# Fused attention and feed-forward: q and k turned by VectorE, first-half row sums added by GpSimd, V's first store moved

## The chip, the cores and the metric

The kernel runs on one NeuronCore of one Trainium2 chip. The time is device microseconds (us) of one execution; the time before is 1375.58 us, the median of 3 runs (1372.02 to 1378.19).

Names used throughout: PE is TensorE, DVE is VectorE, ACT is ScalarE, POOL is GpSimd, SP is SyncE, which here only issues DMAs. PEld is TensorE's weight load.

## The reference

Two batches of 1024 tokens, 1024 channels, 32 heads of 32. The FFN branch is one product with the signs of a weight.

```
def _L0_attn_ref(hidden_states, Wqkv, q_ln_w, q_ln_b, k_ln_w, k_ln_b, Wout):
    qkv = jnp.einsum('bsd,ed->bse', hidden_states, Wqkv)
    qkv = jnp.clip(qkv, -CLIP_QKV, CLIP_QKV)
    q, k, v = jnp.split(qkv, [D_MODEL, 2 * D_MODEL], axis=-1)
    q = _layer_norm(q, q_ln_w, q_ln_b)
    k = _layer_norm(k, k_ln_w, k_ln_b)
    ...
    scores = jnp.einsum('bqhd,bkhd->bhqk', q, k) * scale
    scores = scores + slopes[None, :, None, None] * rel[None, None]
    scores = jnp.where(causal[None, None], scores, jnp.float32(-1e+30))
    probs = jax.nn.softmax(scores, axis=-1)
    out = jnp.einsum('bhqk,bkhd->bqhd', probs, v).reshape(B, S, D_MODEL)
    return jnp.einsum('bsd,ed->bse', out, Wout)
...
x = L0_attn_hidden_states
xn = _layernorm(x, axis=-1)
x = x + _L0_attn_ref(xn, ...) + _L0_ffn_ref(xn, ...)
```

## The kernel before

The engines run hand-written instruction lists, tied by semaphores; nothing reorders them. `ready(n)` is the count a semaphore has once item n is done, `slot_free(n)` the count at which item n may overwrite item n-2.

**Stages.** PE goes through five products of 16 token tiles each (128 tokens by 1024 outputs): F (the feed-forward), Q, K, V, and at the end the output product. Between V and the output product lies attention. A tile of Q, K or V is 48 matmuls of 512 columns (L1038) into two of four PSUM banks, so product t+2 can begin only once DVE has taken tile t out of its banks.

**The Q and K stages.** In step t, DVE clips product t out of PSUM (L899), computes its mean and variance (L830, L835), splits a piece of the next weight (`split_lo`, L823), and scales and shifts the tile to `u[p]` (L920, L923), for which it needs a factor from POOL (L588). PE then turns the tile, 8 transposes of 128x128 fp32 (`turn_qk`, L1085) that stand behind the next product in PE's list. ACT copies the turned tile to its high half `th` (L718) and stores it; DVE subtracts to get the low half `tl` (`turned_low`, L909), which SP stores (L420). Each store writes runs of 128 tokens, 256 bytes, into `q_scr` or `k_scr`, laid out [head, dim and half, token]. The first product of the next stage waits for the last `split_lo` (`w_lo`).

**The V stage.** DVE clips tile t into one of two buffers (`vst`), and SP stores it (`store_v`, L439); DVE's clip of tile t+2 waits for that store. In SP's list the first of these stores stands behind the loads of the first three stacks (L357). A stack holds what one group of 4 heads needs of q and k, 128 rows with halves, ALiBi terms and a row of maxima; it is loaded in 8 parts, in runs of 1 or 2 KB. The last four V products have the first group's maxima in between.

**Attention.** There are 16 groups (8 of 4 heads in each batch). A group has 12 chunks, c = 0 to 11: c = 0 to 3 are the keys t = 0 to 3 of the first half of the queries, with 512, 384, 256 and 128 columns; c = 4 to 11 are t = 0 to 7 of the second half. At each place (c, j), j a head, PE computes scores (L1169, with a mask product L1172 on the diagonal), then some items of the next group's maxima (L1108; DVE reduces them, L940 and L944; ring of 3 banks), and at places named by `PV_AFTER` the product of an earlier chunk with V (L1192, 4 heads side by side, fp32) and with a matrix of ones (L1197), which gives the softmax's row sums in PSUM. ACT takes the exponential (L760) into one of four slots `p32`, used in turn. In the second half four chunks (t = 1, 2, 3, 5) aren't multiplied with ones: POOL adds them up in `acc` (L619), and one product with ones (L1202) closes the sum. ACT copies the product and the sums out (`os_copy`, L768, L769), SP sends the sums through DRAM for DVE's reciprocal, POOL multiplies (`o_norm`, L598), ACT and POOL split into halves (`o_high` L778, `o_low` L608). Two rows of maxima per group are turned on PE, copied by DVE, and put into the stack by SP (L444, L448). ACT issues the loads of the stack of group n+2 and of V.

## Time and profile before

| | us |
|---|---|
| median of 3 runs (lowest, highest) | 1375.58 (1372.02, 1378.19) |
| the profiled execution | 1374.1 |
| its span in the trace | 1372.3 |
| PE busy in the span | 1330.4 (97%) |
| DVE, ACT, POOL busy | 772.8, 503.8, 481.3 |
| first transpose of a q tile starts at | 167.17 |
| first V product starts at | 510.20 |
| last product of V is clipped from | 705.79 |
| first output product starts at | 1199.66 |

A row of the timeline is start, length, engine, line, operation, output and input, and how many instructions it merges; in brackets is the engine's idle time ahead and what ended it. The chain of waits follows the work that ended last back from the end. A PE that is "busy" has a matmul in flight, so its share says little by itself: what counts is which wait ends last in a stage.

### The profile page before, as it was taken

What the parts mean: (1) busy time and instruction counts of PE and PEld (TensorE: products, weight loads), DVE (VectorE), ACT (ScalarE), POOL (GpSimd) and SP (SyncE); (2) the same over time, 40 slices, a digit from 0 to 9 for tenths busy, and PEclk for the clock granted to TensorE, in tenths of its full rate; (3) what the DMA queues carried; (4) which work ended last, traced back from release to release, by engine and by line L of the source; (5) the groups of instructions that cost most, each with busy time, mean ns of one, the idle gap of its engine ahead of it and who ended that gap; (6) DMA issues with size and microseconds to landing.
All of it is one profiled execution on the core that took longest, in us unless ns stands there. A gap on an engine that the chain in (4) does not pass through costs nothing.

```text
span 1372.3 us, 36304 instructions
## 1 busy us (share of the span) xinstructions
PE 1330.4 (97%) x15012; PEld 687.2 (50%) x15012; DVE 772.8 (56%) x1779; ACT 503.8 (37%) x1019; POOL 481.3 (35%) x328
## 2 busy tenths in 40 slices
PE   5999999999999999699999999999999999999998
PEld 3455444444444444244345566566556565444443
DVE  4664366665666661112678888888888888111111
ACT  6453011111111110000027777777777777700000
POOL 5652000000000000000004556655555566687665
PEclk9999999999999999899999999999999999999999
DMA  6545122222222226722221333333333331334543
GB/s 244 177 170 182 54 67 71 69 69 69 69 69 69 69 69 144 195 70 69 70 63 43 88 95 91 92 89 86 93 89 85 91 96 39 100 134 157 165 138 123
DMA packets 143800, 138.00 MB, mean 101 GB/s; under 512 B 81969, under 2 KB 110769, under 8 KB 143474
## 3 DMA queue, kind: packets, MB, share of 16 engines
q1 hardware_dynamic: 79199, 99.55, 23.8%
q10 hardware_dynamic: 64467, 36.50, 10.3%
q8 instruction: 104, 1.70, 0.5%
q14 instruction: 30, 0.25, 0.1%
HBM read 93.42 MB, written 42.21 MB: 99 GB/s over the span
## 4 chain that ended last, share of the span: by engine, by line
PE 94%; DMA 2%; DVE 2%; SPq 1%; ACT 1%; issue 1%; POOL 0%; DVEq 0%; ACTq 0%; POOLq 0%
PE ps L1038 55%; PE ps L1108 9%; PE ps L1169 9%; PE ps L1192 9%; PE ps L1197 5%; PE ps L1172 2%; PE ps L1085 2%; SPq L357 1%; PE ps L1027 1%; PE ps L1202 1%; DMA v_scr<-arena 1%; DMA arena<-in_k_fill 1%; DMA arena<-in_x 0%; DVE arena L899 0%; DVE small L830 0%
## 5 line engine op out<-in xcount | busy, mean ns | idle before, releaser
L1038 PE MATMUL ps<-arena 128*128 128x512 f16 x3584 | 791.3, 381 | 16.4 <-DVE arena L899 11.2
L1038 PEld LDWEIGHTS ps<-arena 128*128 128x128 f16 (+1 forms) x3584 | 348.5, 98 | 434.3 <-issue 14.5
L760 ACT ACTIVATE arena<-ps 128x512 f32<-128x512 f32 (+3 forms) x768 | 330.7, 498 | 132.4 <-PE ps L1172 81.4
L619 POOL TENSOR_TENSOR arena<-arena 128x2048 f32<-128x2048 f32 (+1 forms) x48 | 201.8, 4204 | 345.6 <-ACT arena L760 343.3
L940 DVE CUSTOM_DVE_ANT_0 ps<-ps,arena 128x128 f32<-128x128 f32 (+3 forms) x512 | 240.3, 518 | 66.0 <-PE ps L1108 63.6
L1169 PE MATMUL ps<-arena 128*32 128x512 f16 (+3 forms) x3072 | 258.9, 326 | 3.0 <-DVE arena L899 1.4
L1108 PE MATMUL ps<-arena 127*32 127x512 f16 (+3 forms) x3072 | 239.7, 327 | 0.2
L668 ACT ACTIVATE arena<-arena 128x512 f32 (+1 forms) x64 | 40.0, 627 | 472.6 <-DMA arena<-in_wqkv_t 313.4
L899 DVE TENSOR_SCALAR arena<-ps 128x1024 f32<-128x1024 f32 x48 | 58.8, 1224 | 216.4 <-PE ps L1038 187.7
L944 DVE TENSOR_REDUCE arena<-ps 128x1 f16<-128x512 f32 x256 | 163.0, 683 | 16.7 <-PE ps L1108 16.7
L1192 PE MATMUL ps<-arena 128*32 128x512 f32 (+3 forms) x1536 | 162.1, 486 | 0.5 <-issue 0.3
L542 POOL TENSOR_TENSOR small<-small 128x1 f32<-128x1 f32 x48 | 19.6, 408 | 407.7 <-DVE small L835 406.0
L1169 PEld LDWEIGHTS ps<-arena 128*32 128x32 f16 x3072 | 99.7, 96 | 73.3 <-ACT arena L760 37.0
L1172 PE MATMUL ps<-arena 128*32 128x128 bf16 x2048 | 125.5, 218 | 0.0
L1108 PEld LDWEIGHTS ps<-arena 127*32 127x32 f16 x3072 | 90.7, 96 | 42.6 <-DVE arena L940 7.2
L1004 DVE SCALAR_TENSOR_TENSOR arena<-ps,arena 128x1024 f32<-128x1024 f32 x16 | 19.6, 1225 | 153.6 <-PE ps L1038 130.8
L1197 PE MATMUL ps<-arena 128*32 128x512 f32 (+3 forms) x1024 | 97.3, 445 | 0.0
L1172 PEld LDWEIGHTS ps<-arena 128*32 128x32 bf16 x2048 | 66.6, 97 | 48.8 <-issue 31.0
L940 DVE DVE_READ_ACCUMULATOR2_ANT arena<- 128x1 f16 x512 | 73.2, 143 | 0.0
L830 DVE BATCH_NORM_STATS2 small<-arena 128x6 f32<-128x512 f32 x96 | 61.6, 684 | 6.1 <-DMA arena<-in_x 5.0
L608 POOL TENSOR_TENSOR arena<-arena 128x512 f16<-128x512 f32 x32 | 37.4, 1169 | 65.0 <-ACT arena L778 65.0
L920 DVE SCALAR_TENSOR_TENSOR arena<-arena,small 128x1024 f32<-128x1024 f32 x32 | 41.1, 1284 | 33.4 <-POOL small L588 33.4
(53 smaller groups left out, 801.4 us busy)
## 6 DMA issues: line engine op xcount, KB each, us to landing
arena<-in_x SPq DMA_DIRECT2D x32, 512.0 KB, 5.2
arena<-in_wqkv_t SPq DMA_DIRECT2D x48, 256.0 KB, 3.0
arena<-k_scr ACTq DMA_DIRECT2D x39, 256.0 KB
base_scr<-arena SPq DMA_DIRECT2D x16, 512.0 KB, 3.0
v_scr<-arena SPq DMA_DIRECT2D x16, 512.0 KB, 2.9
arena<-r_scr SPq DMA_DIRECT2D x32, 256.0 KB
arena<-base_scr SPq DMA_DIRECT2D x16, 512.0 KB, 4.1
out_dram<-arena SPq DMA_DIRECT2D x16, 512.0 KB, 6.1
```

Of the source, the lines that this page charges most:

```text
L619: nc.gpsimd.tensor_tensor(acc[:, :, at:HALF], former, p32[k % PSLOTS][:, :, 0:w], ALU.add)\
L760: nc.scalar.activation(p32[k % PSLOTS][:, j, 0:w], ps[:, TRB[x % RB], 0:w], ACT.Exp, scale=SCALE).then_inc(exp_done, 1)
L830: ins = nc.vector.bn_stats(bst[p][:, 6 * c:6 * c + 6], xc[p][:, c * HALF:(c + 1) * HALF])
L899: nc.vector.tensor_scalar(dst[p], banks(2 * p, 2), lim, -lim, ALU.min, ALU.max)\
L940: ins = nc.vector.tensor_tensor_reduce(tile, tile, mnat[:, HALF - width:HALF], scale=-1.0, scalar=3e38, op0=ALU.add, op1=ALU.min, accum_ou ...
L944: ins = nc.vector.tensor_reduce(negm[s % 2][:, at:at + 1], tile, AX, ALU.max, negate=True)
L1038: ins = nc.tensor.matmul(dst[c], lhs(k, a), wparts[:, k, b, c * HALF:(c + 1) * HALF], start=(k == 0 and (a, b) == order[0]), stop=(k == KT ...
L1108: ins = nc.tensor.matmul(ps[r:r + DH, NATB[use(s, pos) % RB], col:col + width], q[0:P - 1, i // 4, j, at:at + DH], k[0:P - 1, j, key:key + ...
L1169: ins = nc.tensor.matmul(dst, k[:, j, t * P + r:t * P + r + DH], q[:, qb, j, at:at + w], start=True, stop=not diagonal)
L1172: ins = nc.tensor.matmul(dst[:, 0:P], idb[:, r:r + DH], mtr, start=False, stop=True)
L1192: ins = nc.tensor.matmul(dst(O_BANK, j, at), v[:, t, j, :], p[:, j, 0:w], start=first, stop=last)
L1197: ins = nc.tensor.matmul(dst(S_BANK, j, at), ones_w, p[:, j, 0:w], start=first, stop=last and qb == 0)
```

## The change

Three things change.

**q and k.** `turn_qk` and its identity are gone from PE. DVE transposes `u[p]` (fp32) into a new buffer `ut[p]` right after L923, with one instruction that turns each 32x32 block in its place. A partition of the result is then (quadrant a of 32 tokens, dim), a column (head, token in the quadrant). ACT and DVE take the halves from `ut` in place of PSUM. `turned_low` moves ahead of `split_lo` in the step, ACT's `turn_out` ahead of `split_hi`. The steps of Q and K alternate between the batches (`tile=p * QT + j`). The scratch becomes [batch, a, tile, half, dim, head and token]: a store writes runs of 2 KB, a stack load reads runs of 256 bytes, in 5 parts in place of 8. In a stack, the 128 tokens of a tile now lie as 4 pieces of 32 (64 bytes each), 1024 elements apart, so the moving operand of L1108 and L1169 has three dimensions. Each row of maxima goes into the stack by 4 DMAs in place of 1.

**First-half sums.** Chunks 0 to 2 are no longer multiplied with ones. POOL adds chunks 1 and 2 onto chunk 0's slot, in place (`add_first`), and 8 products with ones (`sums_first`) at place (6, 2) replace 12 of them; chunk 3 stays direct. For that the slots get a fixed map (`SLOT`, `HELD`), ACT waits for the additions and for `sums_first` before it reuses them, and `NATS`, `PV_AFTER` and the places of `o_norm` and `o_high` change.

**V's first store.** It moves ahead of the stack loads in SP's list, and these are dealt out 3 at a time over the next V tiles.

The core of the diff:

```diff
         def _(sp):
@@
             sp.wait_ge(fill_ld, 16 * 2 * STACKS)
-            for n in range(STACKS):
-                for part in range(LOADS):
-                    load_part(sp, n, part)
             store_v(0, 0)
             for t in range(2, NT):
                 load_w(WO, t, t % 2, t // 2)
+                for m in range(3 * (t - 2), min(3 * (t - 1), STACKS * LOADS)):
+                    load_part(sp, m // LOADS, m % LOADS)
                 store_v(t - 1, 1 - t % 2)
@@ POOL
+            def add_first(n, c):
+
+                at = span(c)[2]
+                k = n * NC + c
+                pool.wait_ge(exp_done, GH * (k + 1))
+                pool.wait_ge(pv_done, n * NC + 1)
+                need(pool, add0_done, adds0_for(k) - 1)
+                total = slot(0)[:, :, at:HALF]
+                nc.gpsimd.tensor_tensor(total, total, slot(c), ALU.add).then_inc(add0_done, 1)
@@ DVE
                     nc.vector.scalar_tensor_tensor(u[p], u[p], rs[p], b, ALU.mult, ALU.add)\
                       .then_inc(u_done, 1)
-                    if not first:
-                        turned_low(q - 1, 1 - p, (j if p else j - 1) + NT // 2 * (blk - 1))
-                    elif blk == K:
-                        turned_low(q - 1, 1, NT // 2 - 1)
+                    dve.wait_ge(u_done, ready(q))
+                    dve.wait_ge(lo_done, slot_free(q))
+                    nc.vector.transpose(ut[p], u[p]).then_inc(qt_done, 1)
@@ PE
                 def step(t, p, j, first=False):
-                    block_product(blk, t, p)
-                    if blk == K or not first:
-                        turn_qk(t + (NT * (blk - 1) - 1), 1 - p)
+                    block_product(blk, t, p, tile=p * QT + j)
@@
-                    ins = nc.tensor.matmul(dst, k[:, j, t * P + r:t * P + r + DH], q[:, qb, j, at:at + w],
+                    ins = nc.tensor.matmul(by_tile(dst), k[:, r // DH, t, j], tiles_of(q, j, q0, w),
                                            start=True, stop=not diagonal)
@@
+            def sums_first(n):
+
+
+                pe.wait_ge(add0_done, ADDS0 * (n + 1))
+                for cols in (slice(0, (ADDS0 + 1) * P), slice((ADDS0 + 1) * P, HALF)):
+                    for j in range(GH):
+                        ins = nc.tensor.matmul(ps[j * DH:(j + 1) * DH, S_BANK, cols], ones_w, slot(0)[:, j, cols],
+                                               start=False, stop=cols.start > 0)
+                ins.then_inc(sums0_done, 1)
```

DVE's list in a step of the Q and K stages, before (L899 clip, L830 and L835 statistics, L823 `split_lo`, L920 and L923 scale and shift, L909 `turned_low`):

```order
L899 TENSOR_SCALAR arena<-ps 128x1024
L916 REGISTER_ALU
L830 BN_STATS small<-arena 128x6 x2
L823 ISA x2
L823 SCALAR_TENSOR_TENSOR arena<-arena 128x512
L835 BN_AGGR small<-small 128x2
L920 SCALAR_TENSOR_TENSOR arena<-arena,small 128x1024
L923 SCALAR_TENSOR_TENSOR arena<-arena,small 128x1024
L907 REGISTER_ALU
L909 TENSOR_TENSOR arena<-ps,arena 128x1024
```

The same step now (L940 clip, L950 `turned_low`, L864 `split_lo`, L976 the transpose):

```order
L940 TENSOR_SCALAR arena<-ps 128x1024
L957 REGISTER_ALU
L871 BN_STATS small<-arena 128x6 x2
L950 TENSOR_TENSOR arena<-arena 128x1024
L864 ISA x2
L864 SCALAR_TENSOR_TENSOR arena<-arena 128x512
L876 BN_AGGR small<-small 128x2
L969 SCALAR_TENSOR_TENSOR arena<-arena,small 128x1024
L972 SCALAR_TENSOR_TENSOR arena<-arena,small 128x1024
L974 REGISTER_ALU
L976 STREAM_TRANSPOSE arena<-arena 128x1024
```

One instruction is added at the end of the step, and `turned_low` stands before `split_lo`.

SP's list at the start of the V stage, now, from the last fill of the stacks (L506), with the names of the waits; before, all 24 parts of the loads (L357 there) stood between the last fill and the first V store (L439 there):

```order
L506 DMA arena<-in_k_fill 32x4096
L458 DMA v_scr<-arena 128x1024 [waits mm_out,fill_ld]
L405 DMA arena<-in_wout_t 128x512 [waits w_lo,w_hi]
L375 DMA arena<-k_scr 32x32x128
L375 DMA arena<-k_scr 64x32x128
L375 DMA arena<-in_k_extra 3x4096
L458 DMA v_scr<-arena 128x1024 [waits mm_out]
```

The V store (L458) now comes first, and it still waits for the fills.

PE's list around `sums_first` (L1248) in a group, now: scores L1206, maxima L1151:

```order
L1206 MATMUL ps<-arena 32x512 [waits exp_done]
L1206 MATMUL ps<-arena 32x512 x3
L1151 MATMUL ps<-arena 32x512 [waits nat_out]
L1151 MATMUL ps<-arena 32x512 x3
L1248 MATMUL ps<-arena 32x384 [waits add0_done]
L1248 MATMUL ps<-arena 32x384 x3
L1248 MATMUL ps<-arena 32x128 x4
L1206 MATMUL ps<-arena 32x512 [waits exp_done]
```

PE has a new wait there, on POOL's additions; all later scores of the group stand behind it.

## Rows read from the trace of the kernel before

**Rows 1.** The page: busy time and share of each engine.

```profile
PE 1330.4 (97%) x15012; PEld 687.2 (50%) x15012; DVE 772.8 (56%) x1779; ACT 503.8 (37%) x1019; POOL 481.3 (35%) x328
```

**Rows 2.** The chain of waits, in order of time: start, length, what.

```profile
167.17 0.87 PE ps L1085 x8
168.04 10.36 PE ps L1038 x48
...
495.60 0.87 PE ps L1085 x8
```

**Rows 3.** Timeline of one step of the Q stage, DVE's rows.

```profile
268.31 1.22 DVE L899 TENSOR_SCALAR arena<-ps 128x1024 f32<-128x1024 f32 x1 [2.78 <-PE ps L1038]
...
274.27 1.28 DVE L923 SCALAR_TENSOR_TENSOR arena<-arena,small 128x1024 f32<-128x1024 f32 x1
275.47 1.22 DVE L909 TENSOR_TENSOR arena<-ps,arena 128x1024 f16<-128x1024 f32 x1
```

**Rows 4.** Groups by line and shape: the same subtraction with both inputs in SBUF.

```profile
L852 DVE TENSOR_TENSOR arena<-arena 128x1024 f16<-128x1024 f32 x16 | 18.9, 1184 | 3.9 <-ACT arena L687 3.9
```

**Rows 5.** The chain of waits at K's first product, and from K's last to V's first.

```profile
327.80 10.53 PE ps L1038 x48
...
506.87 1.24 DVE arena L899
...
509.45 0.70 DVE arena L823
...
510.20 12.23 PE ps L1038 x48
```

**Rows 6.** Timeline of the V stage's start.

```profile
537.92 2.02 SPq L357 DMA_DIRECT2D arena<-k_scr  x3
...
553.53 0.43 SPq L439 DMA_DIRECT2D v_scr<-arena  x1
...
564.29 1.22 DVE L899 TENSOR_SCALAR arena<-ps 128x1024 f32<-128x1024 f32 x1 [28.70 <-DMA v_scr<-arena]
...
565.57 34.60 PE L1038 MATMUL ps<-arena 128*128 128x512 f16 x152 [11.19 <-DVE arena L899]
```

**Rows 7.** Windows: length, busy PE, PEld, DVE, ACT, POOL, clock, DMA share, GB/s.

```profile
189.60:234.57 44.97, 44.97 (x227) 22.43 (x226) 28.09 (x32) 6.17 (x8) 2.97 (x8) 1.00 0.29 71
...
744.09:775.08 30.99, 30.99 (x686) 18.69 (x682) 26.03 (x87) 23.54 (x55) 17.37 (x7) 1.00 0.34 90
```

**Rows 8.** Windows just after two of PE's idle times, same columns.

```profile
510.20:514.30 4.10, 4.10 (x12) 1.54 (x13) 3.13 (x4) 0.00 (x0) 0.74 (x2) 0.58 0.29 66
...
565.50:569.00 3.50, 3.43 (x9) 1.26 (x10) 2.53 (x4) 0.66 (x2) 0.00 (x0) 0.52 0.75 262
```

**Rows 9.** Timeline, PE in a group of attention, from chunk 0's products on.

```profile
743.91 1.04 PE L1192 MATMUL ps<-arena 128*32 128x512 f32 x8
...
744.77 1.04 PE L1197 MATMUL ps<-arena 128*32 128x512 f32 x8
...
753.20 0.42 PE L1169 MATMUL ps<-arena 128*32 128x512 f16 x4
```

**Rows 10.** Timeline, ACT and POOL in a later group.

```profile
878.67 1.62 ACT L760 ACTIVATE arena<-ps 128x512 f32<-128x512 f32 x3
...
879.39 9.26 POOL L619 TENSOR_TENSOR arena<-arena 128x2048 f32<-128x2048 f32 x2 [8.70 <-ACT arena L760]
...
889.85 3.47 POOL L619 TENSOR_TENSOR arena<-arena 128x1536 f32<-128x1536 f32 x1
```

**Rows 11.** Timeline of POOL in the output stage: dependent operations of 1024 columns.

```profile
1206.22 2.35 POOL L638 TENSOR_TENSOR arena<-arena 128x1024 f32<-128x1024 f32 x1 [2.03 <-DMA arena<-alpha_scr]
1208.65 2.36 POOL L640 TENSOR_TENSOR arena<-arena 128x1024 f32<-128x1024 f32 x1
```

**Rows 12.** Window over most of the last group, columns as in Rows 7.

```profile
1166.00:1190.00 24.00, 21.37 (x418) 10.25 (x414) 5.11 (x15) 18.23 (x45) 10.59 (x7) 1.00 0.16 48
```

**Rows 13.** DMA issues: KB each, median us from issue to landing.

```profile
arena<-v_scr ACTq DMA_DIRECT2D x14, 512.0 KB, 4.1
```

More of the change, by code:

```diff
@@ L112, in build_program @@
         xl = [f16(split_at + s * DM + DM // 2, DM) for s in range(2)]
+        ut = [f32(split_at + s * DM, DM) for s in range(2)]
         at += 2 * DM
@@ L916, in qk_step, with between @@
                     dve.wait_ge(mm_out, ready(g))
-                    statistics(g, p, lambda: split_lo(blk + 1, t, p, j))
+                    def between():
+                        if not first:
+                            turned_low(q - 1, 1 - p, (j if p else j - 1) + NT // 2 * (blk - 1))
+                        elif blk == K:
+                            turned_low(q - 1, 1, NT // 2 - 1)
+                        split_lo(blk + 1, t, p, j)
+                    statistics(g, p, between)
                     dve.wait_ge(rstd_done, ready(g))
```

211 lines of the change are left out of this document (112 added, 99 removed).

## The prediction

> **What bounds the kernel now.** I read the page first: PE has work in flight 97% of the span [rows 1]. That says who is busy, not who waits, so I went on to the chain of waits, stage by stage.
>
> In the Q and K stages the chain is PE alone: a product of 10.36 us, the 8 transposes 0.87 us, the next product; a step takes 11.24 us [rows 2]. DVE starts its clip, ends `turned_low` 8.38 us later (275.47 + 1.22 - 268.31), and then idles 2.8 us for PE [rows 3]. At the end of a stage the chain leaves PE: clip, statistics, `split_lo`, then the next stage's first product [rows 5].
>
> In the V stage PE stands still for 11.19 us. DVE's clip had waited 28.7 us for the first V store, which SP issued at 553.53 only, behind the stack loads, and which took until 564.29 [rows 6].
>
> In attention a group takes 30.99 us, and PE is busy in all of them, DVE in 26.03, ACT 23.54, POOL 17.37 [rows 7]. The last group, without maxima, is different: PE is busy 21.37 of 24 us [rows 12], so there it waits.
>
> **The transposes.** PE loses 29 sets of 0.874 us that stand on the chain (14 in Q, 15 in K, at one step's distance from 167.17 to 495.60, leaving out the boundary between them), 25.3 us [rows 2]. Two more stand under the waits at the stage ends and give nothing. The last, behind V's first product, cost 0.7 us. Together 26.0 us.
>
> DVE pays. Its step grows by one instruction that the trace does not hold: T for a transpose of 128x1024 fp32. From below, the nearest row is the clip with 1.22 us, from above two passes of 1.28 (L923), 2.56 us [rows 3]. `turned_low` is only moved, and costs 1.18 for 1.22 as it now reads SBUF [rows 4]. DVE's step is thus 8.4 + T plus some 0.1 us of waits on itself. It stays under PE's 10.36 up to T = 1.9. I take T = 1.25, the value of the rows nearest in shape: each pass over 1024 fp32 columns in the step takes 1.22 to 1.28; then DVE's step is 9.75 us and nothing of it shows. ACT's copy needs T's end, about 0.6 us ahead of the next clip, and takes one pass; `turned_low` asks for it 2.5 us after the clip's start. With T = 2.56 the step is 11.05, and 29 steps gain 0.19 us each, 5.5 us in place of 25.3.
>
> The Trainium skill ("VectorE: DVE Perf Modes", The three transpose paths) gives 311 ns for a 128x128 bf16 transpose on VectorE; eight of them are, by that page, an estimate of 2.5 us, the upper case. Its "Vector Engine (DVE) Microarchitecture Reference" (The reshape front-end and per-opcode configuration) says one element per cycle per lane, which speaks for the lower. No run here shows either yet.
>
> At the two stage ends `turned_low` now stands ahead of the `split_lo` that PE waits for: 2 x 1.18 = 2.4 us lost [rows 4]. PE's idle time there grows from 2.5 us to 4.5 or so. What follows such idleness is seen in two places: V's first product took 12.23 us for 10.36 at a granted clock of 0.58 in its first 4.1 us; K's first took 10.53 [rows 5, 8]. I charge both with the long form: 1.7 us more. Bounds 0 and 3.7.
>
> **V's first store.** It still waits for the fills, after which SP had begun the stack loads at 537.92. Issued there, it would land by 548.7 even with the 10.76 us (553.53 to 564.29) that it took behind those loads, and so ahead of the time at which PE stopped (565.57 - 11.19 = 554.4). The whole 11.19 us go [rows 6], and with them the slow clock after it: 0.52 over 3.5 us, 1.7 us [rows 8]. Together 12.9. What comes late next are V stores behind the dealt-out loads; each has two products, over 20 us, while the whole queue of 18 loads held the first one 10.76.
>
> **The stack loads** now come in runs of 256 bytes: 192 rows x 32 = 6144 packets a group. The steps of Q and K write runs of that size: four steps wrote 8 x 1024 packets, besides 4 weight loads, in a DMA share of 0.29 over 44.97 us, 208 us of one DMA engine [rows 7], at most 25 ns a packet. 6144 of them are 154 us, 9.6 us over 16 engines, for a group of 30 us whose share was 0.34 [rows 7]. V's loads in runs of 512 bytes land within 4.1 us for 512 KB [rows 13]. Loads go out a group ahead, so I take nothing. The Trainium skill ("DMA: Bandwidth & Descriptors") wants at least 512 B for line rate, and so speaks against such loads; by the stores' 25 ns that still fits, and were a read three times as dear, it would decide (rival D).
>
> **The moving operand in pieces of 64 bytes.** No row shows one. Below it can't gain; above I have only a half-rate stream. The contiguous form streams 512 columns in 0.216 us (10.36 / 48) [rows 2]. I take no change.
>
> **First-half sums.** A set of 4 products of w columns takes 0.86 us at 512 [rows 9], in proportion 0.64, 0.43 and 0.21 for less. Before: 0.86 + 0.64 + 0.43 + 0.21 = 2.14. Now: 0.21 for chunk 3, 0.64 + 0.21 in `sums_first`, 1.07. A group gains 1.07 us, if PE waits for nothing new. In the last group PE isn't the limit, and I take 0.2: 15 x 1.07 + 0.2 = 16.2 us.
>
> The new wait is `sums_first` on POOL, with all later scores behind it. PE's window: from the end of chunk 0's product with V, 744.77, to place (6, 3), 753.20, were 8.43 us [rows 9]; less the sums taken out between (0.86 + 0.64 + 0.43), plus one more maxima item (0.2), 6.7 us. POOL's chain: 0.12 to start (the first of three exponentials ends near 878.67 + 0.60, the addition starts at 879.39), 3.47 for 1536 columns, 2.43 for 1024 with its own wait, about 0.15 for the signal: 6.2 us [rows 10, 11]. A margin of 0.5 us, if POOL is free: by adding up its rows in the new order, its work from the group before ends about 4 us into the group, and by the columns ahead of it chunk 0's product ends near 7.6. POOL's load becomes 17.4 + 5.8 = 23.2 of 29.9 us. ACT's exponentials of chunk 5 wait for the first addition (3.75 us after that product, against PE's scores at 3.2 by the columns between), about half a microsecond, which the ring of three banks takes up. DVE has 26.0 of 29.9.
>
> **Sum**, against the profiled execution's 1374.1: - 26.0 + 2.4 + 1.7 - 12.9 - 16.2 = - 51.0, so 1323.1. The median of the runs was 1.5 above the profiled one: 1324.5.
>
> **The rivals.**
>
> A. *DVE becomes the bound of Q and K.* T near 2.56. For it: two passes, and the page's figure above. Against: every pass of this shape in the step takes half. 19.8 us are lost again: 1344.
>
> B. *POOL is late in attention.* The margin is 0.5 us of 6.7. If the addition on top of its own input costs as the 2048-column one (4.63 [rows 10]), the chain is 1.2 longer, PE waits 0.7 us a group, 10 us in all: 1335. If all the gain goes: 1341. Against: the second half adds in place too, at 3.47.
>
> C. *Slower than before: the scattered moving operand.* Scores and maxima stream 2 x 4 x 4608 columns a group (the 4 strips side by side count once), 72 times 512, 15.6 us. From 51 / 16 = 3.2 us a group, 21% more, the change loses; at half rate it is 1324 + 16 x 15.6 = 1574. For it only that no row shows the form.
>
> D. *The small loads fill the queues*, slower too. Even if all of today's share stayed (0.34 x 30.99 x 16 = 169 us of one engine), 6144 packets fit into a group of 29.9 us until (478 - 169) / 6144 = 50 ns each. At 100 ns they alone take 38.4 us a group, for 13 groups: 1324 + 13 x 8.5 = 1435 or more.
>
> E. *The V store doesn't come free*, as its own load queue still holds it: + 12.9, 1337.
>
> **Chances and range.** My forecast (1318 to 1331) 0.66; B 0.15; A 0.08; E 0.02; C 0.04; D 0.02; 0.03 for something between. The unknown clock costs and the last group give 3 us below and 4 above. With B and A in, the range is 1318 to 1345. A measurement of this kernel can tell about 0.5% from no change. Faster 0.93, within 0.5% 0.01, slower 0.06.
>
> **What would show it.** The transpose's row on DVE: under 1.9 us, and PE in products of 10.36 back to back with DVE idle for PE in each step; else DVE's clips follow one another without a wait and products begin 11 us apart. The stage ends: PE idle about 4.5 us, products of 12.2 after it. The V stage: no wait of DVE on the V store, no idle PE. Attention: groups of 29.9 us; a wait of PE's weight load in `sums_first` on POOL would be B. Matmuls of scores and maxima still 0.21 us apart, or C. The DMA share near 0.5, or D. A group over 30.3 us, or a Q step over 10.5, makes the forecast wrong.

## The result

The changed kernel takes 1326.8 us at the median of 4 runs (1323.4 to 1329.6), the kernel before 1376.9 on the same chips (1372.0 to 1378.4): a ratio of 0.9641, with a 95% interval from 0.9607 to 0.9675. The forecast was 1324.5. The profiled execution took 1327.45 us with a span of 1325.4, against 1374.1 and 1372.3 of the kernel before.

The page of the changed kernel, busy time of each engine and its share of the span (TensorE works 41 us less than in [rows 1], VectorE 35 and GpSimd 94 more):

```profile
PE 1289.3 (97%) x14628; PEld 640.9 (48%) x14628; DVE 808.0 (61%) x1811; ACT 510.1 (38%) x1018; POOL 574.8 (43%) x360
```

**The Q step**, VectorE's timeline of one step (start, length, engine, line, operation; in brackets the idle time ahead and who ended it), which answers to [rows 3]:

```profile
258.78 1.25 DVE L976 STREAM_TRANSPOSE arena<-arena 128x1024 f32<-128x1024 f32 x1
260.68 1.22 DVE L940 TENSOR_SCALAR arena<-ps 128x1024 f32<-128x1024 f32 x1 [0.66 <-PE ps L1085]
...
263.26 1.22 DVE L950 TENSOR_TENSOR arena<-arena 128x1024 f16<-128x1024 f32 x1
264.40 0.68 DVE L864 SCALAR_TENSOR_TENSOR arena<-arena 128x512 f32 x1
...
266.22 1.28 DVE L969 SCALAR_TENSOR_TENSOR arena<-arena,small 128x1024 f32<-128x1024 f32 x1 [1.01 <-POOL small L610]
...
268.86 1.25 DVE L976 STREAM_TRANSPOSE arena<-arena 128x1024 f32<-128x1024 f32 x1
```

The transpose costs 1.25 us, and VectorE still waits 0.66 us for TensorE's product at the next clip. Clips follow one another in 10.36 us, for 11.24 before.

**The stage ends and V's start.** TensorE's timeline at the first product of K and at that of V; windows behind both (length, then busy time of TensorE, weight loads, VectorE, ScalarE, GpSimd, with counts, then granted clock, DMA share, GB/s); SyncE's issue of the first V store; VectorE's clip of V's third tile:

```profile
316.94 167.38 PE L1085 MATMUL ps<-arena 128*128 128x512 f16 x768 [4.50 <-DVE arena L864]
488.82 111.49 PE L1085 MATMUL ps<-arena 128*128 128x512 f16 x504 [4.50 <-DVE arena L864]
```

```profile
316.90:320.00 3.10, 3.06 (x8) 1.14 (x9) 2.13 (x3) 0.00 (x0) 0.74 (x2) 0.52 0.45 121
488.80:494.00 5.20, 5.18 (x13) 1.83 (x14) 3.90 (x4) 0.00 (x0) 0.74 (x2) 0.50 0.46 142
```

```profile
520.93 0.35 SPq L458 DMA_DIRECT2D v_scr<-arena  x1
...
524.23 1.22 DVE L940 TENSOR_SCALAR arena<-ps 128x1024 f32<-128x1024 f32 x1 [10.05 <-DMA v_scr<-arena]
```

TensorE idles 4.50 us at each stage end (2.49 before, where the last set of transposes had filled 0.87 us of the wait; [rows 5] show the chain there). After either end it has the lower of its two clock levels, 1.2 GHz, for some time; before, of these two products, only V's first had it [rows 8]. VectorE still waits 10 us for V's first store, but TensorE has two banks ahead and doesn't stop: the 11.19 us of [rows 6] are gone.

**Attention**, windows of two groups, and the shares of the chain over ten groups, before and after. The groups answer to [rows 7]:

```profile
741.55:772.25 30.70, 30.39 (x685) 19.16 (x680) 26.34 (x86) 23.75 (x54) 23.24 (x9) 1.00 0.41 91
802.31:832.36 30.05, 30.05 (x685) 16.75 (x680) 25.63 (x86) 23.55 (x54) 23.24 (x10) 1.00 0.40 92
```

```profile
by line: PE ps L1169 26.1%; PE ps L1108 25.4%; PE ps L1192 25.2%; PE ps L1197 14.6%; PE ps L1172 5.8%; PE ps L1202 2.8%; PE ps L1116 0.2%
```

```profile
by line: PE ps L1206 26.9%; PE ps L1151 26.8%; PE ps L1229 25.8%; PE ps L1235 8.6%; PE ps L1209 5.7%; PE ps L1248 2.9%; PE ps L1239 2.9%; PE ps L1158 0.5%
```

The first of the two lines is the kernel before, where L1197 and L1202 are the products with ones, (14.6 + 2.8)% of 30.99 us = 5.39; the second is the changed one, L1235, L1239 and L1248, 14.4% of 30.05 = 4.33. So 1.06 us a group went, and 1.07 was summed. But the group lost only 0.94, for the maxima and the row turns (L1151 and L1158, before L1108 and L1116) have 0.27 us more of the chain and the rest 0.14 less. From one group's first addition to the next (`add_first`, L651) the first three intervals of this execution are 31.07, 30.71 and 30.70 us, and the later ones 30.05 to 30.06 up to the last, 30.73.

**Where the time went**, by landmarks of the two profiled executions:

| stretch | before | after | difference | forecast |
|---|---|---|---|---|
| start to the first clip of Q | 156.9 | 157.2 | + 0.3 | 0 |
| to V's first product | 353.3 | 331.6 | - 21.7 | - 21.2 |
| V, to its last clip | 195.6 | 182.6 | - 13.0 | - 13.6 |
| to the first product of the output | 493.9 | 481.2 | - 12.6 | - 16.2 |
| to the end | 172.6 | 172.7 | + 0.1 | 0 |

(The forecast's 21.2 is 25.3 less 2.4 and 1.7; V's 13.6 is 12.9 and the 0.7 of one set of transposes.)

### The profile page after: what moved, and what is told of

It reads as the page before. It is cut to its first block, busy times and chain, and to the rows that moved or that the text cites. A ratio compares the mean times of both kernels' runs of the same rounds, so it can differ in the third digit from the quotient of the medians.

```text
span 1325.4 us, 35664 instructions
## 1 busy us (share of the span) xinstructions
PE 1289.3 (97%) x14628; PEld 640.9 (48%) x14628; DVE 808.0 (61%) x1811; ACT 510.1 (38%) x1018; POOL 574.8 (43%) x360
## 4 chain that ended last, share of the span: by engine, by line
PE 94%; DVE 2%; DMA 1%; issue 1%; POOL 1%; ACT 1%; SPq 0%; DVEq 0%; ACTq 0%; POOLq 0%
PE ps L1085 59%; PE ps L1151 9%; PE ps L1206 9%; PE ps L1229 9%; PE ps L1235 3%; PE ps L1209 2%; PE ps L1074 1%; PE ps L1248 1%; PE ps L1239 1%; DMA arena<-arena 1%; DVE ps L988 1%; DMA arena<-in_x 0%; POOL arena L651 0%; SPq L470 0%; DVE arena L940 0%
## 5 line engine op out<-in xcount | busy, mean ns | idle before, releaser
L1206 PE MATMUL ps<-arena 128*32 128x512 f16 (+3 forms) x3072 | 256.8, 327 | 3.6 <-DVE arena L940 1.4
L1151 PE MATMUL ps<-arena 127*32 127x512 f16 (+3 forms) x3072 | 237.8, 328 | 0.6 <-DVE arena L988 0.4
L641 POOL TENSOR_TENSOR arena<-arena 128x2048 f32<-128x2048 f32 (+1 forms) x48 | 202.8, 4226 | 37.5 <-ACT arena L793 35.0
L651 POOL TENSOR_TENSOR arena<-arena 128x1536 f32<-128x1536 f32 (+1 forms) x32 | 93.8, 2930 | 262.5 <-PE ps L1229 190.0
L992 DVE TENSOR_REDUCE arena<-ps 128x1 f16<-128x512 f32 x256 | 166.7, 687 | 47.8 <-PE ps L1151 47.7
L1229 PE MATMUL ps<-arena 128*32 128x512 f32 (+3 forms) x1536 | 160.6, 486 | 0.5 <-issue 0.3
L940 DVE TENSOR_SCALAR arena<-ps 128x1024 f32<-128x1024 f32 x48 | 58.8, 1224 | 144.0 <-PE ps L1085 133.9
L1206 PEld LDWEIGHTS ps<-arena 128*32 128x32 f16 x3072 | 93.0, 96 | 76.5 <-issue 28.3
L751 ACT ACTIVATE arena<-arena 128x1024 f16<-128x1024 f32 x32 | 33.8, 1056 | 247.2 <-DVE arena L976 247.2
L1209 PE MATMUL ps<-arena 128*32 128x128 bf16 x2048 | 120.7, 218 | 0.0
L1151 PEld LDWEIGHTS ps<-arena 127*32 127x32 f16 x3072 | 83.9, 96 | 51.8 <-issue 14.6
L1209 PEld LDWEIGHTS ps<-arena 128*32 128x32 bf16 x2048 | 63.1, 97 | 47.1 <-issue 27.6
```

What stands on the lines that cost most here:

```text
L641: nc.gpsimd.tensor_tensor(acc[:, :, at:HALF], former, slot(c), ALU.add).then_inc(add_done, 1)
L651: nc.gpsimd.tensor_tensor(total, total, slot(c), ALU.add).then_inc(add0_done, 1)
L940: nc.vector.tensor_scalar(dst[p], banks(2 * p, 2), lim, -lim, ALU.min, ALU.max)\
L992: ins = nc.vector.tensor_reduce(negm[s % 2][:, at:at + 1], tile, AX, ALU.max, negate=True)
L1151: ins = nc.tensor.matmul(by_tile(dst), q[0:P - 1, r // DH, i, j], tiles_of(k[0:P - 1], j, key, width), start=True, stop=True)
L1206: ins = nc.tensor.matmul(by_tile(dst), k[:, r // DH, t, j], tiles_of(q, j, q0, w), start=True, stop=not diagonal)
```

## The experiments

Twelve kernels follow; each median is of 4 or 5 runs. The start of the kernel up to the first clip, the same code in all, took between 154.3 and 159.0 us in the profiled executions, so parts are compared between landmarks of the trace: A is the time from the first clip of Q to the last of V (548.8 before, 514.2 changed), B from there to the output's first product (493.9 before, 481.2 changed). The kernel before, run beside them, had medians of 1374.0 to 1377.3, so differences of 3 us between medians say nothing by themselves.

**1. How near VectorE is to being the bound.** [rows 3] gave T only by bounds.

```
-                    nc.vector.transpose(ut[p], u[p]).then_inc(qt_done, 1)
+                    nc.vector.transpose(ut[p], u[p]).then_inc(dup_done, 1)
+                    dve.wait_ge(dup_done, q + 1)
+                    nc.vector.transpose(ut[p], u[p]).then_inc(qt_done, 1)
```

> The changed kernel with VectorE's transpose of each q and k tile done twice; the second overwrites the first with the same values, so one transposed tile costs about 2.5 us of VectorE instead of 1.25. Theory (a step's length is TensorE's 10.36 us as long as VectorE's chain is shorter, and VectorE has 0.66 to 0.94 us to spare in a step, its wait for the product): the extra 1.245 us and some 0.07 us for waiting between the two exceed that by 0.4 to 0.65 us in each of 29 to 30 steps, a step becomes 10.75 to 11.0 us, and the kernel about 1339 to 1346 us, nearly all of it between 140 and 490 us. Rival 1 (VectorE's slack is larger than the wait shows, because its wait of 1.01 us for GpSimd inside the step shrinks too): the step stays under 10.5 us and the kernel within 3 us of 1326.8. Rival 2 (VectorE was already the bound of the step): the whole 1.31 us per step, +38 us, about 1365.

1337.1 us (+10.2), A = 524.8 (+10.6). VectorE's timeline across two steps:

```profile
250.79 1.25 DVE L977 STREAM_TRANSPOSE arena<-arena 128x1024 f32<-128x1024 f32 x1
252.07 1.25 DVE L979 STREAM_TRANSPOSE arena<-arena 128x1024 f32<-128x1024 f32 x1
253.24 1.19 DVE L941 TENSOR_SCALAR arena<-ps 128x1024 f32<-128x1024 f32 x1
...
261.66 1.25 DVE L977 STREAM_TRANSPOSE arena<-arena 128x1024 f32<-128x1024 f32 x1
262.94 1.25 DVE L979 STREAM_TRANSPOSE arena<-arena 128x1024 f32<-128x1024 f32 x1
264.11 1.19 DVE L941 TENSOR_SCALAR arena<-ps 128x1024 f32<-128x1024 f32 x1
```

Clip follows transpose without a wait: VectorE is the bound. Steps are 10.87 and 10.59 us in turn, 10.73 in the mean, 0.37 above 10.36; 28 of them are 10.4. The time is 2 us below the range expected; the mechanism holds. VectorE's own chain is thus 10.73 - 1.28 = 9.45 us with one transpose, and a step would have stayed at 10.36 up to a T of about 2.2 us (1.25 + 10.36 - 9.45), not 1.9 as forecast. Rival A, at 2.56, would have cost some 11 us by this (0.40 in each of 28 steps), not 20. Eight times the 311 ns that the Trainium skill ("VectorE: DVE Perf Modes", The three transpose paths) gives for 128x128 bf16 would be 2.5; for 128x1024 fp32, turned in 32x32 blocks, the trace has half of it.

**2. The sums undone, the layout kept.**

```
-        NATS = [3, 4, 3, 4, 3, 4, 4, 4, 5, 3, 2, 3]
+        NATS = [3, 4, 3, 4, 2, 5, 3, 5, 4, 4, 3, 2]
-        DIRECT = [t not in (ADDED if qb else (0, 1, 2)) for qb, t in CHUNKS]
+        DIRECT = [qb == 0 or t not in ADDED for qb, t in CHUNKS]
-        FIRST_ADDS = {3: [1, 2]}
+        FIRST_ADDS = {}
-        SLOT = [(0, 0), (1, 0), (2, 0), (2, 2 * P), (3, 0), (1, 0), (2, 0), (0, 0), (3, 0), (1, 0), (2, 0), (2, 2 * P)]
+        SLOT = [(c % PSLOTS, 0) for c in range(NC)]
```

(with `PV_AFTER`, `HELD` and the places on GpSimd and ScalarE as in the kernel before, and without `sums_first` and its copy)

> The changed kernel with the first-half sums as in the kernel before: every first-half chunk has its own product with ones on TensorE, four equal slots for the exponentials, the old placement of V's products and of the maxima; transposes, the new layout of q and k and V's early store stay. The group then shows what the new layout alone does to it. Theory A (the layout costs the group nothing; the gain of 0.94 us a group that was seen, where 1.07 was forecast, lost its 0.13 to the new order of the maxima and products): a group of 30.99 us as before the change, 15 groups, and since the third to first groups were at 30.7, a total of about 1326.8 + 12.6 = 1339.4. Theory B (the 0.13 us is the layout's: its transfers of 256 B packets or the scattered operands): a group of 31.12 us, about 1341.4. A group of 31.3 or more would say that the layout costs more and hid behind the gain.

1341.8 us (+15.0), A = 514.4 (+0.1), B = 494.5 (+13.2). Windows of two groups:

```profile
847.38:878.38 31.00, 31.00 (x690) 17.45 (x686) 26.10 (x86) 23.46 (x55) 17.43 (x7) 1.00 0.41 90
878.38:909.38 31.00, 31.00 (x690) 17.45 (x686) 26.21 (x86) 23.46 (x55) 17.38 (x8) 1.00 0.40 91
```

Theory A by the trace: with the new layout, its 256 B packets and a DMA share of 0.40 for 0.34, a group takes 31.00 us, against 30.99 in [rows 7]. The layout costs a steady group nothing. By the total alone one would have chosen B: 1.7 us of the 15.0 lie in the kernel's start, 158.9 us here and 157.2 there. And B is 0.6 us longer than in the kernel before, with the same order and sums: in the first group a weight load of TensorE waits 0.5 us for the row of maxima, which now goes in four transfers (experiment 6). In the kernel before nobody waits for it.

**3 and 4. V's first store, undone, and alone.** In the first all 15 transfers of the stacks go ahead of the store again:

```
+            for m in range(STACKS * LOADS):
+                load_part(sp, m // LOADS, m % LOADS)
             store_v(0, 0)
             for t in range(2, NT):
                 load_w(WO, t, t % 2, t // 2)
-                for m in range(3 * (t - 2), min(3 * (t - 1), STACKS * LOADS)):
-                    load_part(sp, m // LOADS, m % LOADS)
```

> The changed kernel with all the transfers of three stacks (15 now) issued ahead of the first store of V, as before the change (24 then). Theory (the forecast's term: the store of tile 0 is queued behind the stack transfers, VectorE's clip of tile 2 waits for its landing and TensorE stands for the bank): TensorE idles at V's third product again, 11.2 us or more, since the same bytes now go in packets of 256 B, plus about 1.7 us of slow clock behind it: +12.9 at the least, 1339.7, and up to +20 (1347) if these transfers are slower by half. Rival (VectorE waited 10.05 us for this store in the changed kernel without TensorE standing still, so the store is not what held V): within 3 us of 1326.8.

The second is the kernel before with the inverse of this edit (24 transfers there) and nothing else.

> The kernel before, with one edit: V's first store is issued ahead of the stack transfers, and these (24 of them) are dealt out three at a time between the later weight loads and stores. Theory (parts are independent, this one is worth the 11.19 us of idle and 1.7 us of slow clock behind it): -12.9 us, about 1364.0 against 1376.9. Rival (the stack transfers now land too late for the maxima that lie in V's last four tiles, or the dealing holds SyncE's queue so that a later store is late): under 8 us gained, with TensorE waiting in V for a stack or for a bank.

Undone: 1344.6 us (+17.8); from V's first clip to its last 188.7 us for 169.4, 19.3 more. TensorE's row at V's third product, and SyncE's issue of the store behind 15 transfers that began at 518.48:

```profile
547.52 52.74 PE L1085 MATMUL ps<-arena 128*128 128x512 f16 x233 [16.84 <-DVE arena L940]
```

```profile
518.48 1.12 SPq L375 DMA_DIRECT2D arena<-k_scr  x2
...
538.11 2.92 SPq L375 DMA_DIRECT2D arena<-q_scr  x2
541.08 1.14 SPq L458 DMA_DIRECT2D v_scr<-arena  x1
```

Alone: 1361.0 us against 1375.6 (ratio 0.9896, 0.9875 to 0.9917), and from V's first product to its last clip 12.98 us less; the sum had 12.9. The rest of the 14.6 lies mostly in the kernel's start, 154.7 us for 156.9. So this part is worth its price by itself, and in the changed kernel it is worth more (19.3 us), for the new transfers are slower to issue: 15 of them hold SyncE's queue 22.6 us, where 24 of the old ones held it 15.6 (537.92 to 553.53 in [rows 6]). With the old order of the stores the changed kernel would have idled 5.65 us longer here than the kernel before (16.84 - 11.19).

**5. The row of maxima behind the last item.** The 0.13 us a group that are missing come with the new sums then: with their order, or with the waits that they bring. One wait of it is longer than before: TensorE's weight load for the transposed row, 0.40 us at the start of a group.

```
-        NATS = [3, 4, 3, 4, 3, 4, 4, 4, 5, 3, 2, 3]
+        NATS = [3, 4, 3, 4, 3, 4, 4, 4, 5, 3, 3, 2]
```

> The changed kernel with one item of the next group's maxima moved from the last chunk of a group to the chunk before it (3 and 2 items there instead of 2 and 3), nothing else. The new layout alone left the group at 31.00 us, so the 0.13 us that are missing from the 1.07 forecast come with the new order. Theory (part of it is TensorE's wait for the row of maxima that follows the last item: 0.40 us at the start of each group, 0.2 us in the kernel before): that wait falls to 0.2 us and the group from 30.05 to 29.85 to 29.95 us, 1 to 3 us in all: about 1325. Rival (the wait is covered, since the engine issues ahead; the 0.13 us lie in the different phase of V's products and maxima all over the group): 30.05 stays, and the time within 1 us, or the group grows since the last scores are then denser elsewhere.

1330.1 us (+3.2, but B is 481.0 for 481.2); the group takes 30.12 us, a little more, and the wait is as it was. What TensorE's weight loads waited for from 805 to 1100 us, in total, times, longest, in the changed kernel and in this one:

```profile
PEld ps L1158 <- DVE arena L988: 3.6, 9, 0.4
```

```profile
PEld ps L1158 <- DVE arena L988: 3.4, 9, 0.4
```

The theory falls: moving the item didn't shorten the wait, and the group didn't shrink.

**6. The first three groups.** In the profiled execution of the changed kernel they take 31.07, 30.71 and 30.70 us. In each, the chain goes through the row of maxima of the second half, which now is four DMAs in place of one. The third of them (start, length, what):

```profile
735.92 0.46 DVE ps L988
736.53 0.56 SPq L470
737.13 0.59 SPq L470
737.77 0.58 SPq L470
738.39 3.98 DMA arena<-arena
742.41 0.62 PE ps L1206 x8
```

```
-        NATS = [3, 4, 3, 4, 3, 4, 4, 4, 5, 3, 2, 3]
+        NATS = [4, 4, 3, 4, 3, 4, 4, 4, 5, 3, 2, 2]
```

> The changed kernel with one item of the next group's maxima moved from the last chunk of a group to its first (4 items there instead of 3, 2 at the end instead of 3). The row of maxima for the second half is then turned one score earlier, and the chunk that needs it comes one item later, some 0.8 us more room for its four transfers. Theory (the first three groups take 30.7 instead of 30.05 us because TensorE waits there 0.6 us for this row, a term the forecast's sum did not hold): all groups are at 30.05 or less and the time falls by 3 x 0.65 = 2.0 us, to about 1324.9. Rival (the first three groups are longer for another reason, such as the transfers for V and the stacks at that point): they stay at 30.7. A second way to miss: the margin of GpSimd's first-half sums, 0.65 us, is eaten or widened by the move.

1334.9 us (+8.1), nearly all groups 30.6 us, two of them 31.7 (B = 489.7). This move takes the place of one wait by others: VectorE now ends the idle time of the row's weight loads by up to 1.1 us.

```profile
PEld ps L1158 <- DVE arena L998: 5.1, 9, 1.1
```

It neither shows nor refutes the row's part. The other profiled executions do, those of the six kernels whose attention code is that of the changed one (experiments 1, 3 and 8 to 11). The second and third interval are 30.03 to 30.07 us in all six, and 30.71 and 30.70 only here; here the row took 4.0 us from the last issue to landing in each of the three groups. So these two waits are real, cost 2 x 0.65 = 1.3 us in this trace, and the other executions don't have them.

The wait in the very first group is no accident of one execution. In experiments 1, 3, 9 and 10 its row takes 4.1 to 4.2 us, TensorE's weight load waits 1.0 to 1.1 us for it, and the interval is 30.95 to 31.07 us. Experiment 9 has:

```profile
675.93 4.13 DMA arena<-arena
680.11 0.62 PE ps L1214 x8
```

In experiment 8 the row landed in 3.25 us and in experiment 11 the chain doesn't pass through it; there the interval is 30.31 and 30.15 us. So the first group's row costs 0.9 to 1.0 us in most executions, and with the two later ones 2.3 us here.

**7. GpSimd late by a known amount.** The forecast gave the first-half sums a margin of 0.5 us at `sums_first`. In the trace the second addition ends at 838.40 (836.01 + 2.39). The weight load of the product, which is what waits for it, starts at 838.66, and the product itself at 838.88: 0.26 and 0.48 us later. (The expectation's 0.65 goes by the chain, which counts the product from 839.06, the end of the matmuls before it.)

```profile
836.01 2.39 POOL L651 TENSOR_TENSOR arena<-arena 128x1024 f32<-128x1024 f32 x1 [0.17 <-POOL arena L651]
838.66 0.34 PEld L1248 LDWEIGHTS ps<-arena 128*32 128x32 f32 x8
```

```
                 total = slot(0)[:, :, at:HALF]
+                if c == 1:
+                    for i in range(3):
+                        nc.gpsimd.tensor_tensor(spare, ones, ones, ALU.add).then_inc(spare_done, 1)
+                        pool.wait_ge(spare_done, 3 * n + i + 1)
```

> The changed kernel with three additions of 128 columns (of ones, into columns nobody reads) on GpSimd ahead of its two first-half additions in each of the 16 groups. By the two sizes of the first-half additions (3.48 us for 1536 columns, 2.38 for 1024: 2.1 ns a column and some 0.2 us for the operation) one takes about 0.47 us: the additions end 1.4 us later in each group. In the changed kernel they end 0.65 us ahead of the product with ones that waits for them. Theory (rival B's mechanism: TensorE has nothing else ahead of that product, and what GpSimd is late beyond 0.65 us comes onto the group): each group grows by 0.7 to 0.8 us, 30.05 to about 30.8, and the kernel by 10 to 13 us, to 1337 to 1340, with TensorE's waits showing GpSimd as the releaser some 15 times. Rival (TensorE takes the scores and maxima behind it in the same time, or the additions only start when the product with V is done and so can shift): under 3 us.

1346.0 us (+19.1), where 1337 to 1340 were expected: the group takes 31.34 to 31.36 us, +1.30 for a delay of 1.43. Who waited is another than expected. GpSimd, then ScalarE at the exponentials of chunk 5, then TensorE's scores:

```profile
835.69 1.35 POOL L654 TENSOR_TENSOR arena<-arena 128x128 f32<-128x128 f32 x3 [4.31 <-ACT arena L799]
837.12 3.47 POOL L657 TENSOR_TENSOR arena<-arena 128x1536 f32<-128x1536 f32 x1
```

```profile
840.67 1.58 ACT L799 ACTIVATE arena<-ps 128x512 f32<-128x512 f32 x3 [1.67 <-POOL arena L657]
```

```profile
841.32 0.40 PE L1212 MATMUL ps<-arena 128*32 128x512 f16 x4 [1.12 <-ACT arena L799]
```

ScalarE can't write chunk 5 before the first addition has read its slot, and of the 1.43 us only 0.13 don't reach the group, in spite of TensorE's ring of three banks. In the changed kernel the same two rows are these:

```profile
832.36 3.49 POOL L651 TENSOR_TENSOR arena<-arena 128x1536 f32<-128x1536 f32 x1 [4.42 <-ACT arena L793]
```

```profile
835.93 1.58 ACT L793 ACTIVATE arena<-ps 128x512 f32<-128x512 f32 x3 [0.26 <-PE ps L1206]
```

The addition ends at 835.85 and ScalarE starts at 835.93, 0.08 us later. That looks like a small margin, but it is none. With GpSimd late, where ScalarE certainly waits for it, the distance is the same 0.08 to 0.09 us in all groups read: it is the time from the addition's end to ScalarE's start. In the changed kernel it is 0.08 or 0.09 (once 0.07) in every group from the fourth on. The trace names TensorE's scores as the releaser, but those of this exponential (the first of its four) began at 835.05 and took 0.40, so they were done at 835.45:

```profile
835.05 0.40 PE L1206 MATMUL ps<-arena 128*32 128x512 f16 x4
```

ScalarE thus waits for GpSimd in every steady group of the changed kernel already. How long is told by experiment 12, where the addition ends some 0.65 us ahead of ScalarE: ScalarE's idle time at this place is 0.18 us there and 0.25 here, so GpSimd holds it by less than 0.1 us.

**8 to 11. The stage ends.** First the clock behind them, with the idle time filled by 18 products into an unused bank:

```
+            def keep_busy():
+                for i in range(18):
+                    nc.tensor.matmul(ps[:, 6, :], xnt[:, 0, 0, 0, :],
+                                     xnt[:, 0, 0:2, :, :].rearrange("p k s c -> p (k s c)"), start=True, stop=True)
...
+                if blk == K:
+                    keep_busy()
                 pe.wait_ge(w_lo, ready(NT * blk - 1))
...
+            keep_busy()
             pe.wait_ge(w_lo, ready(NT * V - 1))
```

> The changed kernel with 18 more products of 512 columns on TensorE at each of the two stage ends (Q to K and K to V), ahead of its wait for the last low half of the weights; they go to a bank nobody reads and take 18 x 0.216 = 3.9 us of the 4.50 us in which TensorE would stand. Theory (the slow clock behind a stage end, 0.52 granted in the 3.1 us behind 316.9 and 0.50 in the 5.2 us behind 488.8, comes from that standing): both stretches run at 1.00 and the time falls by 1.5 + 2.6 = 4.1 us at the most, to about 1322.7; the gap between the clips of the last tile of a stage and the first of the next falls from 16.5 and 17.7 us to about 15. Rival (the clock falls for another reason, or falls anyway): the gaps stay as they are, 1326.8, or grow by up to 4 us each if the added products themselves run at half the clock.

1323.0 us (-3.8), A = 510.2 (-4.0). Windows behind the two ends, in columns as above:

```profile
318.27:321.30 3.03, 3.03 (x14) 1.38 (x15) 2.06 (x3) 0.00 (x0) 0.74 (x2) 1.00 0.48 123
489.20:494.40 5.20, 5.20 (x26) 2.37 (x25) 3.81 (x3) 0.00 (x0) 0.47 (x1) 1.00 0.48 141
```

The clock stays at its upper level, 2.4 GHz, with TensorE's idle time down to 0.62 us. The slow stretches came with TensorE's standing still: with the same waits and the same work around them they are gone.

Then the order in the last step: `split_lo` ahead of `turned_low` (and `split_hi` ahead of `turn_out` on ScalarE).

```
                     def between():
+                        if last:
+                            split_lo(blk + 1, t, p, j)
                         if not first:
                             turned_low(q - 1, 1 - p, (j if p else j - 1) + NT // 2 * (blk - 1))
...
-                        split_lo(blk + 1, t, p, j)
+                        if not last:
+                            split_lo(blk + 1, t, p, j)
```

> The changed kernel with one order changed in the last step of Q and of K: VectorE makes the low half of the weights ahead of the low half of the turned tile (and ScalarE the high halves in the same order). The forecast's term was 2 x 1.18 us for that place, plus 1.7 us of slow clock for both. Theory: TensorE's idle at the two stage ends falls from 4.50 to about 3.4 us and the time by 2.3 us, and up to 2 us more where the clock then stays up: 1322.5 to 1324.5. Rival (the low half of the weights then waits for ScalarE or for the load of the weights instead): under 1 us gained.

1323.6 us (-3.2), A = 511.1 (-3.2). TensorE's idle is 3.37 us at both ends, 2.3 us less in all; the other 0.9 us are a shorter slow stretch behind V's first product.

Then `split_lo` directly behind the clip (ScalarE's order as in the edit before):

```
                     clipped(g, p, xc)
+                    if last:
+                        split_lo(blk + 1, t, p, j)
```

> The changed kernel with the low half of the weights moved further forward in the last step of Q and of K: behind the clip, ahead of the statistics (1.29 us) and of the turned tile's low half (1.14 us), with ScalarE's high half of the weights first. With the low half behind the statistics TensorE's idle was 3.37 us and the time 1323.6. Theory: the idle falls to 2.1 to 2.5 us (it ends at ScalarE's high half of the weights, 1.6 us after the clip's start, or at the clip's end), and the time by 2 x 1.0 us more, to about 1321.5, more if the clock then stays up. Rival (VectorE's own chain of that tile, now 0.7 us later, holds the first step of the next stage, or the load of the last weights comes out on top): no gain over 1323.6.

1319.3 us (-7.5), A = 509.5 (-4.7), idle 2.46 and 2.42 us, with the clock at 0.59 and 0.70 in the 3 us behind; 2.7 of the 7.5 us lie in the start of the kernel (154.5 us for 157.2). The low half now waits 0.41 to 0.45 us for ScalarE's high half.

And both together, with 10 products in place of 18:

> The kernel with the low half of the weights behind the clip at both stage ends, and with 10 products of 512 columns (2.16 us) at either stage end, into a bank nobody reads, in what idle is left to TensorE. Theory (idle and slow clock are two separate costs of a stage end: 18 such products took away 3.8 us of 1326.8 with the idle left as it was; the order takes away the idle): the gap from the last clip of a stage to the first of the next falls from 16.5 and 17.7 us to 12.5 to 13, the time by 8 to 9 us, to 1318 to 1319, the best of all. Rival (the slow clock is gone with the shorter idle anyway, so the added products bring nothing): the same as without them, about 1321.5.

1318.8 us (-8.0; ratio to the kernel before 0.9592, 0.9571 to 0.9613), A = 505.9 (-8.3). The distance between the clips across a stage end is 12.9 us, for 16.5 and 17.7 in the changed kernel and 14.7 without the added products. So by the trace the two costs are separate and both go; the medians of 1319.3 and 1318.8 don't separate the last two kernels, since the first one's start was 2.9 us quicker in its profiled execution; A does, by 3.6 us. By A this is the fastest kernel of the case.

**12. The additions sooner.** On top of the last kernel:

```
-        PV_AFTER = {(0, 2): [-2], (2, 1): [-1], (3, 0): [0], (4, 2): [1], (5, 2): [2], (5, 3): [3],
+        PV_AFTER = {(0, 2): [-2], (2, 0): [-1], (2, 3): [0], (4, 2): [1], (5, 2): [2], (5, 3): [3],
...
-                            if (c, j) == (2, 1):
+                            if (c, j) == (2, 0):
                                 os_copy(n - 1, 1)
```

> The kernel with the low half of the weights behind the clip and 10 added products at either stage end (1318.8 us, groups of 30.06 us), and in the group: the last product with V of the group before, ScalarE's copy of its result and the first product with V of the group each placed one score earlier (chunk 2, scores 0 and 3, instead of chunk 2, score 1, and chunk 3, score 0). GpSimd's first-half additions start when that first product ends, and their first one ends 0.08 us ahead of ScalarE's exponentials that need its slot: a margin that the forecast did not name, which the run with GpSimd 1.43 us late made visible (group +1.30). Theory A (that margin is also what the missing 0.13 us of the group are): the additions start some 0.4 us sooner, the group falls to about 29.95 us, and the kernel by 1 to 2 us, to 1317. Theory B (as long as nobody waits for GpSimd the margin costs nothing): the additions end some 0.4 us sooner, the group stays within 0.03 of 30.06 and the time within 1 us of 1318.8. Theory C (the result bank of V's products is then not free in time, or the additions of the group before come late for the product with ones): the group grows by 0.1 to 0.4 us.

1325.2 us (+6.4 to the kernel it builds on), B = 488.6 (+7.9), groups of 30.6 us, 0.55 more: theory C, at a price above the 0.4 that it named. ScalarE's copy of the result comes ahead of exponentials and waits there for TensorE, 0.85 us for 0.50:

```profile
823.17 0.60 ACT L805 ACTIVATE arena<-ps 128x512 f32<-128x512 f32 x1 [0.85 <-PE ps L1255]
```

At chunk 5 ScalarE no longer waits for GpSimd (the addition there ends at 828.66):

```profile
829.34 1.09 ACT L797 ACTIVATE arena<-ps 128x512 f32<-128x512 f32 x2 [0.18 <-issue]
```

But whether that wait costs the changed kernel's group anything can't be read from a group that grew by another; this stays open.

## Why the prediction was right

**The transposes: right.** 25.3 us off the chain, T = 1.25 against 1.245 measured, DVE with time to spare. Only its margin was off, and on the safe side: 0.9 us of room in the step (experiment 1) in place of 0.6. That T was 1.25 and not 2.56 was a choice between two values that no row could make; the forecast said so, and rival A stood for the other.

**The stage ends: right, somewhat short.** Idle 4.50 us, as said. The distances between clips across the two ends grew from 13.89 and 15.70 to 16.48 and 17.67, 4.6 us in all; the sum had 2.4 + 1.7 = 4.1. The wait for `split_lo` grew by 1.14 us at each, 2.3 in all, which is the time from `turned_low`'s start to the next instruction's (263.26 to 264.40); the operation itself takes 1.225 us as before, not the 1.18 of [rows 4]. The slow clock took the other 2.3, 1.5 at K's first product and 0.8 at V's, which had been slow before and got slower.

**V's first store: right.** 12.98 us alone, 12.9 forecast. The forecast didn't say that the transfers, if left ahead, would have become dearer.

**Layout, small packets, scattered operand: right.** A group of 31.00 us with them, 30.99 without (experiment 2). A score's matmul of 512 columns takes 380 ns; before, 379 (groups by line and shape, from 700 to 1100 us; the kernel before first):

```profile
L1169 PE MATMUL ps<-arena 128*32 128x512 f16 x1240 | 120.0, 379 | 1.4 <-DVE arena L899 1.4
```

```profile
L1206 PE MATMUL ps<-arena 128*32 128x512 f16 x1264 | 123.0, 380 | 0.3 <-DMA arena<-arena 0.2
```

The Trainium skill ("DMA: Bandwidth & Descriptors", Specifications) wants 512 B at least in a transfer for line rate, and so spoke against the loads. Beside a steady group's work the trace shows no cost of them; where they stood on the path, ahead of V's store in experiment 3, it is in line with the page: 5.65 us more of idle time. No run changed the packets' size alone.

**The first-half sums: right in mechanism, 3.6 us too large.** That is nearly the whole miss of the sum. In the landmarks B fell by 12.6 us, not 16.2. Three terms make it up, within 0.1 us:

- 15 x 0.13 = 2.0 us less are the steady groups: the products with ones gave their 1.07 us, and the chain's part of the rest grew by 0.13. Experiment 2 places it in the new sums, not in the layout, and experiments 5 and 6 show that single items, moved, shift the group between 30.05 and 30.6 us. They don't say whether the 0.13 come from the order or from ScalarE's wait for GpSimd, which by its size (under 0.1 us) could be a part of it but not all; this stays open.
- Some 2.3 us less are the first groups, where the row of maxima came late (experiment 6). This term was missing in the sum: the text said that a row now takes four transfers and gave them no price, although the wait for the row has all scores of the second half behind it.
- About 0.6 us more are the last group, which gave 0.8 in place of 0.2 (from the second-half addition of 1536 columns of the last group but one, L619 before and L641 now, to the first output product: 30.9 us for 30.0).

By the forecast's own sign, a group over 30.3 us, the first three groups and the last interval stand against it; the steady ones, at 30.05, bear it out.

**The margin of GpSimd: right by luck in part.** At `sums_first` it was 0.26 us to the weight load and 0.48 to the product, for 0.5 forecast. The forecast also named the nearer reader, ScalarE's chunk 5, with about half a microsecond of wait: between the end of its scores and its start the trace has 0.48. But it let the ring of banks take up half a microsecond, and experiment 7 shows that of a further delay only 0.13 us in 1.43 are lost on the way. ScalarE already waits for GpSimd in each steady group, so GpSimd had no time to spare there, and of 1.43 us more on it 1.30 came onto the group. Rival B was closer than its 0.15 said, and it would have come through ScalarE, not through the product with ones.

## What to carry to other kernels

A wait that another engine feeds has as many margins as it has readers: write down for each buffer that an added operation holds who needs it next, and take the smallest; here a ring of three banks passed on 1.30 of 1.43 us. A releaser that the trace names can be the wrong one of two: a distance that stays the same to 0.01 us from group to group, behind the end of another engine's work, gives the right one away. Where an engine hands over between stages, put what the next stage waits for ahead of everything else in the last step, and count its idle time with the slow clock behind it: here 9.0 us of the one and 4.0 of the other (experiment 8). And compare landmarks of the trace with the same work between them before a difference of 2 us in the medians is given a cause.

## What was not expected of the hardware

- The clock behind idle time. Idle of 2.4 to 4.5 us at a stage end was followed by 3 to 5 us at granted clocks of 0.50 to 0.70 (1.2 GHz for the most part), also where it was no longer than 2.42 us. With 0.62 us of idle or less, it stayed at 1.00. K's first product in the kernel before had 2.49 us of idle ahead and no slow stretch [rows 5]; what told these two apart isn't known.
- Issuing transfers of 256 B packets back to back: 15 took SyncE 22.6 us, some 1.5 us each, while 24 transfers of larger runs took 15.6 us, 0.65 each.
- Four transfers of 1 KB in place of one of 4 KB: 3.1 us from issue to landing at the median for 2.0, and 1.9 us go by before the fourth is issued (736.53 to 738.39 in experiment 6).
- The start of the kernel, up to the first clip of Q, took 154.3 to 159.0 us with the same code in 14 profiled executions: most of the scatter of the totals.
